# Three PSUM banks for one layer's scores, and the causal zeroing cut into halves

## The chip, the cores and the metric

The kernel is one program on one core of a Trainium2 chip. The metric is the device time of one execution in microseconds (us).

## The reference

The input x is 8 batches of 512 rows by 128 columns. Two layers follow each other, each with a layer normalisation ahead of it and x added behind it. Cut to what matters:

```
# layer A (16 heads, head size 8, values of 32)
Q = heads(x); K = heads(x @ Wk + bk); V = heads(x @ Wv + bv)
attn = softmax(Q K^T + causal mask)
x + gelu(concat(attn @ V)) @ Wf + bf
# layer F (8 heads, size 64, 8 experts)
q = x @ w_q; k = x @ w_k; gates = sigmoid(x @ w_gate); sel = argmax(gates)
gm = onehot(sel) * gates
values = sum_e gm[e] * (x @ value_experts[e])
out = softmax(causal(q k^T / 8)) @ values
sum over heads and experts of gm[e] * (out @ output_experts[e])
```

## The kernel before

Five engines run written-out programs, ordered among themselves and held together by semaphores. The batches go one after the other: layer A's attention, its end (`turn`: gelu and projection back, L814), layer F's projections and expert values, layer F's attention. Work of neighbouring batches is woven in: during layer F's attention the first maximum units of the next batch's layer A run, and during layer A's attention the expert products (L698) of the layer F before.

Layer A's 16 heads make four groups of four. Softmax takes two passes. In the first a *maximum unit* is a score block (queries in the partitions) in one of the two banks ps_max0, ps_max1; VectorE takes maxima (L1310), ScalarE the sums of exponentials (L919). VectorE makes from both, for each query, minus maximum minus logarithm of the sum (L1315 on), TensorE transposes it (`maxima_transposed`, L626), ScalarE copies it to mt_a (`maxima`), and three DMAs on the SP queue carry it into rows of the stacked queries (L395). In the second pass a *score unit* (`score_unit`, L587) computes scores with the keys in the partitions; the rows just made are part of that matmul. ScalarE's exponential (`weights`, L970) brings it into pt, already normalised. Each group has three stages of four units (512, 384 and 256 + 128 columns), so a batch has 48 units in layer A. When all four heads of a stage are there, GpSimd zeroes what lies above the diagonal (L1177), and TensorE weighs the values with it (`weigh`, L678), one stage behind the scores.

Units 0 to 23 of layer A alternate between ps_exp0 and ps_exp1, so unit u waits for the exponential of unit u-2. From unit 24 (WIDE) on the maximum units are done and the two ps_max banks are scores' banks too. The bank ps_m0 is used for transposes and for one value tile. Maximum units of the last group are spread over score units 2 to 22 (LATE). Lists give the places of the products by score unit: STEPS_AT holds the steps at which VectorE makes a product's operand and TensorE does the product before it, PRODUCTS_AT further ones of TensorE, LAST_AT of VectorE. VALUE_AT and SUMS_AT place the value tiles and the last sums of layer F among the maximum units ahead of the scores.

Of the kernel before, what the change touches and what calls it, by code (L numbers as in the profile page):

```python
# [24 lines left out]
P = 128  # L25
# [81 lines left out]

SCORES_AT = 10

# [4 lines left out]

VALUE_AT = {2: 0, 3: 1, 5: 2, 7: 3}

# [54 lines left out]
def build(nc, x, wk, bk, wv, bv, wf, bf, wq, wkf, wg, ve, oe, ident, consts, out):  # L171
    ctx = ExitStack()
    with ctx:
# [124 lines left out]
        mrow = {k: [sem(f"mrow{k}{n}", 2 * 16 * MROWS[k]) for n in range(2)] for k in "AF"}  # L298
        causal, pv_done = K2("causal", NST, NST), K2("pv_done", NST, NST)
        sums_out = K2("sums_out", GROUPS - 1, GROUPS)  # L300
# [189 lines left out]
        def _(pe):  # L490
# [131 lines left out]
            def maxima_transposed(k, b, g):  # L622
                dst = free(k, "T", g, (t_done[k], b, g + 1))
                pe.wait_ge(neg_ready[k].sem, neg_ready[k].count(b, g + 1))
                if k == "A":
                    nc.tensor.transpose(dst[:].bitcast(BF16)[0:48, 0:P], nm_a[:, g % 2, :], ident_b[:]  # L626
                                        ).then_inc(t_ready[k].sem, 1)
                else:
                    nc.tensor.transpose(dst[0:16, 0:P], nm_f[:, g % 2, :], ident_sb[:]).then_inc(t_ready[k].sem, 1)

            def score_unit(k, b, g, s, j):

                u, h = (g * STAGES + s) * HG[k] + j, g * HG[k] + j
                if k == "A" and u in (WIDE + 2, WIDE + 3):
                    pe.wait_ge(max_done["A"].sem, max_done["A"].count(b, UNITS["A"]))
                elif u >= 2:
                    pe.wait_ge(exp_done[k].sem, exp_done[k].count(b, u - 3 if k == "A" and u >= WIDE + 4 else u - 1))
                elif k == "A":
                    pe.wait_ge(va.sem, va.count(b, T))
                else:  # L640
                    pe.wait_ge(chosen.sem, chosen.count(b, choices(T * E - 1 + u)))
# [75 lines left out]
            def attention_a(a):  # L717
# [3 lines left out]
                for n, (g, m) in enumerate(pre_units(a)):  # L721
                    if a > 0 and n < 2:
                        continue
# [4 lines left out]
                    if g == 2 and m == SCORES_AT:  # L728
                        rows_arrived(a, 0)
                        score_unit("A", a, 0, 0, 0)  # L730
                        score_unit("A", a, 0, 0, 1)
                    max_unit("A", a, g, m)
# [6 lines left out]
                for g in range(GROUPS):  # L739
                    if g > 0:  # L740
                        rows_arrived(a, g)
                    for s in range(STAGES):
                        n = g * STAGES + s
                        for j in range(HG["A"]):
                            u = n * HG["A"] + j
                            if u >= 2:
                                score_unit("A", a, g, s, j)
# [6 lines left out]
                            elif u in PRODUCTS_AT:  # L754
                                product(a - 1, PRODUCTS_AT[u])
                            if s == 1 and j == 0 and g + 1 < GROUPS:
                                maxima_transposed("A", a, g + 1)
                        if n > 0:
# [4 lines left out]
            def attention_f(f):  # L763
# [30 lines left out]
                if f + 1 < B:  # L794
                    value_a(f + 1, 0)
                    for g, m in pre_units(f + 1)[:2]:
                        if m == 0:
# [60 lines left out]
        def _(act):  # L858
# [27 lines left out]
            def maxima(k, b, g):  # L886
                act.wait_ge(t_ready[k].sem, t_ready[k].count(b, g + 1))
                src = ps_m[BANK[(k, "T", g)]]
                if mrow[k][g % 2].count(b, 16 * MROWS[k] * (g // 2)):
                    act.wait_ge(mrow[k][g % 2].sem, mrow[k][g % 2].count(b, 16 * MROWS[k] * (g // 2)))  # L890
                if k == "A":
                    copy(mt_a[:, g % 2, :], src[:].bitcast(BF16)[0:48, 0:P]).then_inc(t_done[k].sem, 1)
                else:
                    copy(mt_f[:, g % 2, :], src[0:16, 0:P]).then_inc(t_done[k].sem, 1)

# [77 lines left out]
            def attention(k, b):  # L973
                n_units = STAGES * HG[k]
                for g, m in pre_units(b) if k == "A" else ():
                    if g == 2 and m == SCORES_AT:
                        weights(k, b, 0, 0)
                        weights(k, b, 0, 1)
                    denominators(k, b, g, m)
# [14 lines left out]
                for g in range(GROUPS):  # L994
                    for s in range(STAGES):
                        n = g * STAGES + s
                        for j in range(HG[k]):
                            u, m = n * HG[k] + j, s * HG[k] + j
                            if k == "F" or u >= 2:
                                weights(k, b, n, j)  # L1000
# [12 lines left out]
                            if k == "F" and b + 1 < B:  # L1013
                                firsts(b + 1, u - 1)
                            if k == "A" and s == 1 and j == 0 and g + 1 < GROUPS:
                                maxima(k, b, g + 1)
                            if k == "F":
# [129 lines left out]
        def _(pool):  # L1147
# [23 lines left out]
            def attention(k, b):  # L1171
                for n in range(NST):
                    pool.wait_ge(exp_done[k].sem, exp_done[k].count(b, (n + 1) * HG[k]))
                    s0, m = (n % 2) * 4, 2 if n % STAGES == 2 else 1
                    v = pt[:, s0:s0 + HG[k], 0:m * P].rearrange("p h (m c) -> p h m c", c=P)

                    nc.gpsimd.affine_select(out=v, in_=v, compare_op=ALU.is_ge, fill=0.0, base=0,  # L1177
                                            pattern=[[0, HG[k]], [0, m], [1, P]], channel_multiplier=-1
                                            ).then_inc(causal[k].sem, 1)

# [405 lines left out]
```

## Time and profile before

| | |
|---|---|
| median of 3 runs | 1226.84 us (1225.18 to 1228.56) |
| profiled execution, its own time | 1228.14 us |
| its span | 1226.4 us |
| granted TensorE clock, mean | 0.996 |
| busy share TensorE, ScalarE, VectorE, GpSimd | 92%, 77%, 70%, 30% |
| one batch (533.4 to 678.1 of the span) | 144.7 us |
| selects of GpSimd (L1177) | 192 |

The page's busy shares are means over the span; a window or a list of waits shows one stretch. In a timeline row the bracket at the end is the idle time of the engine before it and what ended it. Batches are equal to within some tenths of a microsecond, so one stands for all.

### The profile page before, as it was taken

The page shows a single profiled execution, that of the slowest core. Times are in us where ns is not written, and L with a number is a line of the kernel's source. Part 1 is how long each engine was busy: PE and PEld are TensorE (multiplying, and loading weights), DVE is VectorE, ACT ScalarE, POOL GpSimd, SP SyncE. Part 2 cuts the span into 40 slices and gives each one's busy share as a digit, 9 for nine tenths or more (in the row PEclk, how much of TensorE's full clock was granted, in tenths as well). Part 3 has the DMA queues.
Part 4 walks back from the last instruction along what each step waited for, and adds up shares of the span by engine and source line. Part 5 has one row for each costly group of instructions (what it writes and reads, how often), then busy time and mean ns, then how long its engine had stood idle before and what let it go on. Part 6 is the DMA issues. An engine that isn't in the chain of part 4 may idle for free.

```text
span 1226.4 us, 20153 instructions
## 1 busy us (share of the span) xinstructions
PE 1130.3 (92%) x5846; PEld 644.6 (53%) x5846; DVE 862.7 (70%) x2715; ACT 941.2 (77%) x2639; POOL 364.0 (30%) x460
## 2 busy tenths in 40 slices
PE   5989998999989999899989999899998999989998
PEld 3536753376434764357543675347643575435743
DVE  5735867678765878569676687767876597856844
ACT  3985898858986789867997589876898578986751
POOL 1024314432234223252233421442232432323310
PEclk9999999999999999999999999999999999999999
DMA  5311232022210233003320123202231033300220
GB/s 192 72 69 48 50 108 64 5 61 69 83 53 4 71 87 98 11 3 79 106 71 11 47 51 106 64 5 62 78 88 38 4 79 89 87 3 26 56 71 9
DMA packets 43647, 72.75 MB, mean 59 GB/s; under 512 B 9664, under 2 KB 25408, under 8 KB 43216
## 3 DMA queue, kind: packets, MB, share of 16 engines
q1 hardware_dynamic: 42142, 66.95, 20.3%
q10 hardware_dynamic: 1394, 4.50, 1.4%
q8 instruction: 47, 0.77, 0.3%
q14 instruction: 64, 0.52, 0.1%
HBM read 45.34 MB, written 8.80 MB: 44 GB/s over the span
## 4 chain that ended last, share of the span: by engine, by line
PE 64%; ACT 15%; DVE 12%; issue 5%; DMA 2%; POOL 1%; SPq 1%; ACTq 0%; DVEq 0%; POOLq 0%
PE ps_m L698 15%; PE ps_o L678 10%; ACT masked L919 7%; ACT pt L970 6%; PE ps_max L587 5%; PE ps_exp L587 4%; DVE masked L1310 4%; PE ps_m L496 3%; PE ps_exp L589 3%; PE ps_exp L496 3%; PE ps_m L498 3%; PE ps_m L497 3%; PE ps_exp L498 2%; PE ps_max L814 2%; PE ps_exp L497 2%
## 5 line engine op out<-in xcount | busy, mean ns | idle before, releaser
L1310 DVE CUSTOM_DVE_ANT_0 masked<-ps_max,mask 128x512 f32<-128x512 f32 (+3 forms) x768 | 350.1, 487 | 169.5 <-PE ps_max L587 101.2
L919 ACT ACTIVATE masked<-masked,low 128x512 f32<-128x512 f32 (+3 forms) x768 | 423.1, 554 | 52.4 <-DVE low L1310 50.8
L1177 POOL TENSOR_SCALAR_AFFINE_SELECT pt<-pt 128x512 f32<-128x512 f32 (+2 forms) x192 | 143.6, 748 | 556.1 <-ACT pt L970 556.1
L970 ACT ACTIVATE pt<-ps_exp 128x384 f32<-128x384 f32 (+1 forms) x480 | 237.4, 517 | 75.7 <-PE ps_exp L587 48.3
L678 PE MATMUL ps_o<-pt,val 128*32 128x128 f32 (+6 forms) x1536 | 178.7, 445 | 6.8 <-POOL pt L1177 6.8
L698 PE MATMUL ps_m<-at,oe_sb 128*128 128x512 f32 x300 | 154.3, 601 | 1.9 <-DVE at L1361 1.8
L919 ACT ACTIVATION_READ_ACCUMULATOR masked<-masked,low 128x1 f32 x768 | 147.2, 192 | 0.0
L587 PE MATMUL ps_max<-s2k,s1q 72*128 72x512 bf16 (+3 forms) x512 | 121.7, 304 | 21.3 <-DVE low L1310 14.0
L1361 DVE TENSOR_TENSOR at<-osb,hots 128x512 f32<-128x512 f32 x150 | 103.2, 689 | 29.8 <-PE ps_m L698 29.8
L587 PE MATMUL ps_exp<-s1q,s2k 75*128 75x384 bf16 (+3 forms) x384 | 90.7, 304 | 30.8 <-ACT pt L970 30.5
L678 PEld LDWEIGHTS ps_o<-pt,val 128*32 128x32 f32 (+1 forms) x1536 | 51.7, 117 | 106.8 <-issue 75.2
L589 PE MATMUL ps_exp<-s1q,s1k 128*128 128x256 f32 (+2 forms) x256 | 97.1, 390 | 11.0 <-DVE val L1501 9.4
L587 PEld LDWEIGHTS ps_max<-s2k,s1q 72*128 72x128 bf16 x512 | 45.9, 98 | 109.0 <-DVE low L1310 56.5
L698 PE MATMUL ps_m<-kept,oe_sb 128*128 128x512 f32 x212 | 101.1, 596 | 0.0
L1191 POOL CAST s1q<-pt 64x512 fp32r<-64x512 f32 x64 | 41.9, 655 | 166.4 <-ACT pt L1059 163.6
L1501 DVE COPY_PREDICATED val<-osb,ps_m 128x512 f32<-128x512 uint32 x112 | 80.6, 738 | 8.2 <-ACT val L859 8.2
L587 PEld LDWEIGHTS ps_exp<-s1q,s2k 75*128 75x128 bf16 x384 | 28.1, 97 | 108.0 <-ACT pt L970 80.1
L589 PE MATMUL ps_max<-s1k,s1q 128*128 128x256 f32 (+2 forms) x256 | 82.1, 332 | 1.3 <-DVE low L1310 1.3
L589 PEld LDWEIGHTS ps_exp<-s1q,s1k 128*128 128x128 f32 x256 | 48.1, 188 | 65.1 <-issue 39.0
L590 PE MATMUL ps_exp<-s2q,s2k 66*128 66x256 f32 (+5 forms) x256 | 80.4, 325 | 0.0
L590 PE MATMUL ps_max<-s2k,s2q 128*128 128x256 f32 (+5 forms) x256 | 80.1, 324 | 0.0
L1501 DVE COPY_PREDICATED val<-osb,ps_exp 128x512 f32<-128x512 uint32 x112 | 78.3, 736 | 0.3 <-PE ps_exp L498 0.2
(188 smaller groups left out, 2019.4 us busy)
## 6 DMA issues: line engine op xcount, KB each, us to landing
hots<-hot_d SPq DMA_DIRECT2D x48, 256.0 KB, 4.8
s1q<-parts_q SPq DMA_DIRECT2D x96, 96.0 KB
s2k<-parts_k SPq DMA_DIRECT2D x93, 96.0 KB
s1q<-pt SPq DMA_DIRECT2D x64, 128.0 KB, 2.3
s1k<-pt SPq DMA_DIRECT2D x64, 128.0 KB, 2.3
hots<-hot_d ACTq DMA_DIRECT2D x16, 256.0 KB, 4.8
parts_q<-pt SPq DMA_DIRECT2D x24, 128.0 KB, 2.3
parts_k<-pt SPq DMA_DIRECT2D x24, 128.0 KB, 3.9
```

Source lines behind the costliest of these rows:

```text
L496: mm(dst, lh, rh, start=True, stop=False)
L587: return mm(dst, l1[0:n, h, l2], r1[0:n, h, r2], start=True, stop=True)
L589: mm(dst, l1[0][:, h, l2], r1[0][:, h, r2], start=True, stop=False)
L590: return mm(dst, l1[1][n, h, l2], r1[1][n, h, r2], start=False, stop=True)
L678: last = mm(ps_o[g % 2][j * w:j * w + w, qt * P:S], val[:, kt, h * w:h * w + w], pt[:, (n % 2) * 4 + j, c0:c1], start=kt == 0, stop=kt == 3)
L698: mm(ps_m[1][:], oe_sb[:, u], chosen_o(f, u), start=u == 0, stop=u == T * E - 1).then_inc(at_used.sem, 1)
L919: last = nc.scalar.activation(e, e, ACT.Exp, bias=low[:, g % 2, c:c + 1], scale=-1.0, accum_out=den[:, g % 2, c:c + 1])
L970: nc.scalar.activation(pt[:, (n % 2) * 4 + j, 0:c1 - c0], score_bank(k, u)[:, c0:c1], ACT.Exp).then_inc(exp_done[k].sem, 1)
L1177: nc.gpsimd.affine_select(out=v, in_=v, compare_op=ALU.is_ge, fill=0.0, base=0, pattern=[[0, HG[k]], [0, m], [1, P]], channel_multiplier=- ...
L1310: last = v.tensor_tensor_reduce(out=masked[:, u % JUNK, c0:c0 + w], in0=src[:, c0:c0 + w], in1=mask[:, S - w:S], scale=-1.0, scalar=POS, o ...
L1361: v.tensor_tensor(chosen_o(f, u), osb[:, u // E], hots[:, u // E, u % E].bitcast(F8), ALU.mult).then_inc(at_done.sem, 1)
L1501: v.copy_predicated(val[:, t].rearrange("p (h k) -> p h k", k=64), pick, ps_m[BANK[("F", "moe1", n)]][:].rearrange("p (h k) -> p h k", k=6 ...
```

## The change

Layer A's scores of units 0 to 23 go around three banks (ps_exp0, ps_exp1, ps_m0), those from unit 24 on around five. Three scores instead of two are computed ahead, three maximum units instead of two stand ahead of layer F's last weighing. The transposed maxima of groups 1 to 3 no longer have a bank of their own: they are written at column 384 of the bank of a score unit that has 384 columns, two units later than before, and ScalarE copies them once that score is written. Those of group 0 go to ps_exp0. The lists of products, value tiles and last sums are changed. GpSimd's select is cut in two for both layers: each half covers half of a stage's heads and waits only for their exponentials; a weighing waits for both.

```diff
+SCORE_BANKS = {"A": 3, "F": 2}
+BANK["A", "T", 0] = 2
-SCORES_AT = 10
+SCORES_AT, SCORES_FIRST = 10, 3
+BESIDE = ('A',)
+ROWS_WITH = {"A": 2, "F": 0}
-VALUE_AT = {2: 0, 3: 1, 5: 2, 7: 3}
+AHEAD = 3
+VALUE_AT = {3: 0, 4: 1, 6: 2, 8: 3}
-STEPS_AT += [("A", u) for u in (1, 2, 4, 7, 11, 15, 19, 23, 27, 31)]
+STEPS_AT += [("A", u) for u in (1, 3, 5, 7, 10, 13, 16, 19, 23, 27)]
-PRODUCTS_AT = {35: T * E - TURN - 1, 39: T * E - TURN}
-LAST_AT = {(36 + n if n else 33): T * E - TURN + n for n in range(TURN)}
+PRODUCTS_AT = {31: T * E - TURN - 1, 39: T * E - TURN}
+LAST_AT = {(35 + n if n else 31): T * E - TURN + n for n in range(TURN)}
-SUMS_AT = 8
+SUMS_AT = 10
...
-            return (ps_exp + ps_max)[u % 4] if k == "A" and u >= WIDE else ps_exp[u % 2]
+            if k == "A":
+                return (ps_exp + ps_max + ps_m[0:1])[(u - WIDE) % 5] if u >= WIDE else (ps_exp + ps_m[0:1])[u % 3]
+            return ps_exp[u % 2]
+        def rows_unit(k, g):
+            return ((g - 1) * STAGES + 1) * HG[k] + ROWS_WITH[k]
+        def transposed_at(k, g):
+            if g == 0 or k not in BESIDE:
+                return ps_m[BANK[(k, "T", g)]], 0
+            return score_bank(k, rows_unit(k, g)), 384
...
+            def score_bank_free(k, b, u):
                 if k == "A" and u in (WIDE + 2, WIDE + 3):
                     pe.wait_ge(max_done["A"].sem, max_done["A"].count(b, UNITS["A"]))
-                elif u >= 2:
-                    pe.wait_ge(exp_done[k].sem, exp_done[k].count(b, u - 3 if k == "A" and u >= WIDE + 4 else u - 1))
+                elif k == "A" and u >= WIDE + 4:
+                    pe.wait_ge(exp_done[k].sem, exp_done[k].count(b, u - 4))
+                elif u >= SCORE_BANKS[k]:
+                    pe.wait_ge(exp_done[k].sem, exp_done[k].count(b, u + 1 - SCORE_BANKS[k]))
...
-                pe.wait_ge(causal[k].sem, causal[k].count(b, n + 1))
+                pe.wait_ge(causal[k].sem, causal[k].count(b, 2 * n + 2))
...
                         for j in range(HG["A"]):
                             u = n * HG["A"] + j
-                            if u >= 2:
+                            if s == 1 and j == ROWS_WITH["A"] and g + 1 < GROUPS:
+                                maxima_transposed("A", a, g + 1)
+                            if u >= SCORES_FIRST:
                                 score_unit("A", a, g, s, j)
...
             def maxima(k, b, g):
-                act.wait_ge(t_ready[k].sem, t_ready[k].count(b, g + 1))
-                src = ps_m[BANK[(k, "T", g)]]
+                if g == 0 or k not in BESIDE:
+                    act.wait_ge(t_ready[k].sem, t_ready[k].count(b, g + 1))
+                else:
+                    act.wait_ge(s_ready[k].sem, s_ready[k].count(b, rows_unit(k, g) + 1))
+                src, c = transposed_at(k, g)
...
                 for n in range(NST):
-                    pool.wait_ge(exp_done[k].sem, exp_done[k].count(b, (n + 1) * HG[k]))
+                    for half_ in range(2):
+                        w = HG[k] // 2
+                        pool.wait_ge(exp_done[k].sem, exp_done[k].count(b, n * HG[k] + (half_ + 1) * w))
+                        s0, m = (n % 2) * 4 + half_ * w, 2 if n % STAGES == 2 else 1
+                        v = pt[:, s0:s0 + w, 0:m * P].rearrange("p h (m c) -> p h m c", c=P)
+
+                        nc.gpsimd.affine_select(out=v, in_=v, compare_op=ALU.is_ge, fill=0.0, base=0,
+                                                pattern=[[0, w], [0, m], [1, P]], channel_multiplier=-1
+                                                ).then_inc(causal[k].sem, 1)
```

## Rows read from the trace of the kernel before

**Rows 1.** Busy time of each engine over the span, from the page.
```profile
PE 1130.3 (92%) x5846; PEld 644.6 (53%) x5846; DVE 862.7 (70%) x2715; ACT 941.2 (77%) x2639; POOL 364.0 (30%) x460
```

**Rows 2.** Stretches: us, busy PE, PEld, DVE, ACT, POOL, clock, DMA share, GB/s.
```profile
637.00:649.00 12.00, 9.48 (x49) 3.37 (x47) 6.03 (x22) 10.06 (x33) 2.50 (x3) 1.00 0.08 24
649.00:661.70 12.70, 11.51 (x73) 4.09 (x69) 7.60 (x29) 11.50 (x34) 3.31 (x4) 1.00 0.01 1
661.70:678.10 16.40, 15.51 (x123) 6.00 (x122) 11.78 (x25) 13.26 (x29) 7.56 (x8) 1.00 0.02 6
```

**Rows 3.** Waits between 637 and 678.1: who waited for whom, total, times, longest.
```profile
PEld ps_exp L587 <- ACT pt L970: 9.8, 17, 1.3
...
ACT pt L970 <- PE ps_exp L587: 6.0, 7, 1.5
...
PEld ps_o L678 <- POOL pt L1177: 2.3, 3, 1.0
...
PE ps_o L678 <- POOL pt L1177: 0.9, 2, 0.7
```

**Rows 4.** Timeline of TensorE: start, us, what, idle time before it.
```profile
641.28 0.33 PE L587 MATMUL ps_exp<-s1q,s2k 75*128 75x384 bf16 x1
642.61 0.34 PE L587 MATMUL ps_exp<-s1q,s2k 75*128 75x384 bf16 x1 [1.00 <-ACT pt L970]
...
643.00 1.02 PE L698 MATMUL ps_m<-at,oe_sb 128*128 128x512 f32 x2
643.96 1.06 PE L678 MATMUL ps_o<-pt,val 128*32 128x512 f32 x8
644.95 0.50 PE L587 MATMUL ps_exp<-s1q,s2k 75*128 75x256 bf16 x4
```

**Rows 5.** Timeline of ScalarE in the narrow part, exponentials that waited.
```profile
645.39 0.49 ACT L970 ACTIVATE pt<-ps_exp 128x384 f32<-128x384 f32 x1 [1.49 <-PE ps_exp L587]
...
649.58 0.60 ACT L970 ACTIVATE pt<-ps_exp 128x512 f32<-128x512 f32 x1 [0.99 <-PE ps_exp L587]
...
657.36 0.87 ACT L970 ACTIVATE pt<-ps_exp 128x384 f32<-128x384 f32 x2 [0.56 <-PE ps_exp L587]
```

**Rows 6.** Timeline of all engines at the phase's end.
```profile
673.78 0.88 ACT L970 ACTIVATE pt<-ps_max 128x384 f32<-128x384 f32 x2
...
674.12 0.85 PE L678 MATMUL ps_o<-pt,val 128*32 128x384 f32 x8 [0.69 <-POOL pt L1177]
...
674.74 1.44 POOL L1177 TENSOR_SCALAR_AFFINE_SELECT pt<-pt 128x1024 f32<-128x1024 f32 x1 [0.67 <-ACT pt L970]
...
675.98 1.48 ACT L1033 ACTIVATE osb<-osb 128x1536 f32<-128x1536 f32 x1
...
676.23 0.86 PE L678 MATMUL ps_o<-pt,val 128*32 128x256 f32 x16 [0.20 <-POOL pt L1177]
...
677.98 0.50 PE L814 MATMUL ps_max<-wf_sb,osb 128*128 128x128 f32 x3
```

**Rows 7.** Groups of selects by form: busy us, mean ns, idle before them.
```profile
L1177 POOL TENSOR_SCALAR_AFFINE_SELECT pt<-pt 128x512 f32<-128x512 f32 x96 | 77.8, 810 | 301.5 <-ACT pt L970 301.5
...
L1177 POOL TENSOR_SCALAR_AFFINE_SELECT pt<-pt 128x1024 f32<-128x1024 f32 x32 | 38.9, 1215 | 74.6 <-ACT pt L970 74.6
...
L1177 POOL TENSOR_SCALAR_AFFINE_SELECT pt<-pt 128x256 f32<-128x256 f32 x64 | 26.9, 421 | 180.0 <-ACT pt L970 180.0
```

**Rows 8.** The maxima tile: instructions, their ns, and the time to landing.
```profile
L395 SPq DMA_DIRECT2D s1q<-mt_a x96: 502/589/1415, 44.8 to 1099.6; - x96
...
DMA to landing us min/median/max: 1.6/1.7/6.1
```

**Rows 9.** Timeline around the last transposed maxima of layer A.
```profile
662.87 0.34 PE L587 MATMUL ps_exp<-s1q,s2k 75*128 75x384 bf16 x1
...
663.69 0.26 ACT L859 ACTIVATE mt_a<-ps_m 48x128 bf16<-48x128 bf16 x1
...
668.22 0.61 PE L587 MATMUL ps_exp<-s1q,s2k 75*128 75x512 bf16 x2
```

More of the change, by code:

```diff
@@ L640, in score_unit @@
                 else:
-                    pe.wait_ge(chosen.sem, chosen.count(b, choices(T * E - 1 + u)))
+                    pe.wait_ge(chosen.sem, chosen.count(b, choices(min(T * E - 1 + u, T * E))))
+            def score_unit(k, b, g, s, j):
+                u, h = (g * STAGES + s) * HG[k] + j, g * HG[k] + j
+                score_bank_free(k, b, u)
                 dst = score_bank(k, u)
@@ L721, in attention_a @@
                 for n, (g, m) in enumerate(pre_units(a)):
-                    if a > 0 and n < 2:
+                    if a > 0 and n < AHEAD:
                         continue
@@ L729, in attention_a @@
                         rows_arrived(a, 0)
-                        score_unit("A", a, 0, 0, 0)
-                        score_unit("A", a, 0, 0, 1)
+                        for j in range(SCORES_FIRST):
+                            score_unit("A", a, 0, 0, j)
                     max_unit("A", a, g, m)
@@ L755, in attention_a @@
                                 product(a - 1, PRODUCTS_AT[u])
-                            if s == 1 and j == 0 and g + 1 < GROUPS:
-                                maxima_transposed("A", a, g + 1)
                         if n > 0:
@@ L794, in attention_f @@
                 if f + 1 < B:
-                    value_a(f + 1, 0)
-                    for g, m in pre_units(f + 1)[:2]:
+                    for n, (g, m) in enumerate(pre_units(f + 1)[:AHEAD]):
+                        if n == 2:
+                            value_a(f + 1, 0)
                         if m == 0:
@@ L886, in maxima @@
             def maxima(k, b, g):
-                act.wait_ge(t_ready[k].sem, t_ready[k].count(b, g + 1))
-                src = ps_m[BANK[(k, "T", g)]]
+                if g == 0 or k not in BESIDE:
+                    act.wait_ge(t_ready[k].sem, t_ready[k].count(b, g + 1))
+                else:
+                    act.wait_ge(s_ready[k].sem, s_ready[k].count(b, rows_unit(k, g) + 1))
+                src, c = transposed_at(k, g)
                 if mrow[k][g % 2].count(b, 16 * MROWS[k] * (g // 2)):
@@ L891, in maxima @@
                 if k == "A":
-                    copy(mt_a[:, g % 2, :], src[:].bitcast(BF16)[0:48, 0:P]).then_inc(t_done[k].sem, 1)
+                    copy(mt_a[:, g % 2, :], src[:].bitcast(BF16)[0:48, 2 * c:2 * c + P]).then_inc(t_done[k].sem, 1)
                 else:
-                    copy(mt_f[:, g % 2, :], src[0:16, 0:P]).then_inc(t_done[k].sem, 1)
+                    copy(mt_f[:, g % 2, :], src[0:16, c:c + P]).then_inc(t_done[k].sem, 1)
             def repeat_hots(f, p):
@@ L976, in attention @@
                     if g == 2 and m == SCORES_AT:
-                        weights(k, b, 0, 0)
-                        weights(k, b, 0, 1)
+                        for j in range(SCORES_FIRST):
+                            weights(k, b, 0, j)
                     denominators(k, b, g, m)
@@ L998, in attention @@
                             u, m = n * HG[k] + j, s * HG[k] + j
-                            if k == "F" or u >= 2:
+                            if k == "A" and s == 1 and j == ROWS_WITH[k] and g + 1 < GROUPS:
+                                maxima(k, b, g + 1)
+                            if k == "F" or u >= SCORES_FIRST:
                                 weights(k, b, n, j)
@@ L1014, in attention @@
                                 firsts(b + 1, u - 1)
-                            if k == "A" and s == 1 and j == 0 and g + 1 < GROUPS:
-                                maxima(k, b, g + 1)
                             if k == "F":
@@ L1172, in attention @@
                 for n in range(NST):
-                    pool.wait_ge(exp_done[k].sem, exp_done[k].count(b, (n + 1) * HG[k]))
[L1174 to L1179, printed above, removed]
+                    for half_ in range(2):
[6 more added lines that the diff above has]
+                                                ).then_inc(causal[k].sem, 1)
             def copy_rows(f, p):
```

14 lines of the change are left out of this document (8 added, 6 removed).

## The prediction

> **What bounds the kernel now.** I read the page's line of busy times first [rows 1]: TensorE has work in it for 92% of the span, ScalarE for 77%, VectorE for 70% and GpSimd for 30%. An average of that kind does not say which engine a stage waits for, so I cut one of the eight batches into stretches [rows 2]. The change lives in layer A's score phase, in which every score matmul (L587) writes a PSUM bank, ScalarE takes the exponential out of it (L970), GpSimd zeroes what lies above the diagonal (L1177), and TensorE weighs the values with it (L678). In the batch shown this phase runs from 637.0 to 678.1. In its narrow part (units 2 to 23, with two banks for the scores) ScalarE is busy 10.06 of 12.0 us and then 11.50 of 12.7 us, TensorE 9.48 and 11.51 [rows 2]. Neither is full; they take turns. The waits of the phase say why [rows 3]: TensorE's weight loads for scores stood 9.8 us waiting for exponentials to free a bank, and ScalarE's exponentials stood 6.0 us, in seven waits, for scores to arrive. Two engines that wait for each other are short of buffers between them.
>
> How such a wait arises is in the timeline of TensorE [rows 4]. Unit 6's score starts at 641.28. Unit 7's starts only at 642.61, because with two banks it needs the exponential of unit 5. Behind unit 7 in TensorE's order stand a product (643.00) and the weighing of the stage before (643.96), so unit 8's score comes at 644.95. ScalarE runs dry meanwhile and idles 1.49 us before unit 8's exponential at 645.39 [rows 5]. The same happens before units 12 (0.99 us) and 20 (0.56 us) [rows 5]: 3.04 us of the 6.0. The other four waits, 3.0 us together, lie in the wide part (units 24 to 47, already with four banks). There TensorE waits for no exponential; it is full with scores, products and weighings, and its own work sets the pace.
>
> The phase's end is a chain [rows 6]: last exponentials 673.78 to 674.66, the zeroing of four heads at once 674.74 to 676.18, the last weighing at 676.23, then the back projection (L814) at 677.98. Beside it ScalarE, behind its last exponential, loads a table and applies the first gelu from 675.98 to 677.46, which L814 also needs. What follows L814 is paced by TensorE, so a shift of that start moves the batch.
>
> **The change part by part.** *Third bank, narrow part.* Unit u's score now waits for the exponential of u-3. Unit 7 then needs unit 4's exponential, which unit 6 needed before; it can follow right behind unit 6 and its maximum unit, about 641.45 instead of 642.61. The product, weighing and unit 8 follow 1.16 us earlier, and of the 1.49 us idle 0.33 is left before anything else has moved. The 0.99 and 0.56 have the same form and are smaller than one ScalarE unit of work (ScalarE's 21.6 us of narrow work over 22 units make about 1.0 us each), so one bank more covers them. The gain is bounded by 0 below (TensorE merely queues) and 3.04 above (ScalarE never idle). Is TensorE fast enough for the upper end? It has 24.7 us in the narrow part [rows 2] and of these ScalarE's bound is 21.6 (10.06 + 11.50). TensorE's busy sum is 20.99, in which the ends of pipelined matmuls are counted too, and it gets one more product. So both are nearly balanced and some turn-taking stays. I take 2.5 of the 3.04.
>
> *Products moved.* Ten steps at u = 1, 2, 4, 7, 11, 15, 19, 23, 27, 31 become 1, 3, 5, 7, 10, 13, 16, 19, 23, 27, and the extra products at 35 and 39 become 31 and 39. Counted by parts: the wide part had products at 27, 31, 35, 39 and now has them at 27, 31, 39, and the narrow part has one more. A product occupies TensorE from 643.00 until the weighing starts at 643.96, less the gap before it: 0.86 us. In the wide part that is off the pacing engine, in the narrow part it lies in TensorE's former waits. Between 0 and 0.86; I take 0.8. The fifth bank of the wide part removes a wait that isn't there: nothing.
>
> *Zeroing in halves.* Twelve selects of a layer become 24. The forms give the prices [rows 7]: 4x128 columns take 810 ns in the mean, 2x128 take 421, 4x256 take 1215. The first half starts two exponentials earlier, so only the second lies behind the last exponential: 421 instead of 810 ns, and 810 instead of 1215 where the form is wide. GpSimd's total rises by (2 x 421 - 810) = 0.03 to (2 x 810 - 1215) = 0.41 us a stage; for layer F's forms no row shows one head of 128 columns, its price lies between 0 and 421. GpSimd is busy 30%, and its selects waited for exponentials, so the additional time is covered by its idle time. Only five weighings of the phase waited for GpSimd, 3.2 us of queue time and idle [rows 3], most of it at the end: 0.69 us before 674.12 and 0.20 before 676.23 [rows 6]. The last select took 1.44; with a half of 0.81 the last weighing comes 0.63 us earlier and L814 could start at 677.35, but the gelu ends at 677.46. So the tail gains at most about 0.5; I take 0.45, at the least 0.
>
> [...]
>
> *Maxima through a score bank.* The transposed maxima of groups 1 to 3 (L626) are written beside the score of unit j = 2 of the second stage, two units later than now, and ScalarE copies them out only when that score is written. Then three DMAs carry them to the rows that the next group's first score needs. In the wide part this is tight: unit 28's score at 662.87, the copy at 663.69, unit 36's score at 668.22 [rows 9]. The copy moves behind one more exponential, 0.4 us or a little more. Three issues of 0.59 us each put the last 1.2 us behind the first, and 1.7 us later it has landed [rows 8]: 663.69 + 0.5 + 0.27 + 1.2 + 1.7 = 667.4. The need moves to 668.22 - 0.86 = 667.4. I expect 0 to 0.3 us of a new wait in this group and take 0.1; In groups 1 and 2 the need (unit 12, unit 24) comes at the earliest when four more units have passed ScalarE, 3.9 us behind the copy's start, and the rows take 0.27 + 1.2 + 1.7 = 3.2: enough.
>
> [...]
>
> *The rest.* The third maximum unit ahead of the last weighing of layer F, the value tiles one unit later, the sums of layer F two units later and the first three scores at once keep their amount of work. They move between 622 and 637, where VectorE's maxima and ScalarE's sums set the pace and not TensorE. Nothing, at worst 0.3 us a batch either way. The cap in layer F's wait names the same count.
>
> **The sum.** 2.5 + 0.8 + 0.45 - 0.1 = 3.65 us, and a little for units 24 on, which may start up to one ScalarE unit sooner since unit 24 needs unit 21's exponential instead of unit 22's: 3.8 us a batch. Batch 0 has the same phase. 8 x 3.8 = 30 us. The profiled execution took 1228.14 us (span 1226.4), so it becomes 1198; against the median of the three runs, 1226.84, it is 1196.5.
>
> **The rivals.** *Half the gain.* TensorE and ScalarE stay coupled elsewhere: the late maximum units need VectorE and a junk slot, and rows arrive late. Then the narrow part gives 1.3, the move 0.5, the tail 0.2, less 0.1: 1.9 us, 1212. For it speaks that both engines have nearly the same load; against it, that every wait I removed names the bank.
> *No change.* TensorE is at 92% and what it waited for was hidden. Then 1227. Against it speak ScalarE's 6.0 us of idle time at the very waits in question.
> *Slower: rows late.* One maxima landing took 6.1 us instead of 1.7 [rows 8]. If landings behind the later copy took that long, group 3's first score would wait 4.4 us, those of groups 1 and 2 4.4 - 0.7 = 3.7 each: 11.8 - 3.8 = 8.0 us slower a batch, 1290. It decides from a landing of about 3.4 us on, where the three waits together reach 3.8. Against it: DMA is nearly idle in these stretches (share 0.01 to 0.08 [rows 2]).
> *More than forecast.* All upper ends together: 3.04 + 0.86 + 0.5 + 0.4 = 4.8, 1188; and beyond that only if the front part gains too.
>
> **How the numbers follow.** Forecast (1188 to 1204) 0.55, half the gain (1204 to 1219) 0.25, beyond 1188 0.05, no change within 0.3% 0.07, slower 0.08. A measurement of this kernel tells some 0.3% from no change. Faster is then 0.85. The range reaches from 1187 to 1218 and leaves out a little under 2 in 10.
>
> **What would show it.** In the changed profile: waits of ScalarE's exponentials for scores in the phase down from 6.0 to about 2 us, and those of score weight loads for exponentials from 9.8 to under 5; ScalarE's busy share in the narrow part above 93% (87% now); 384 selects, of 421 and about 810 ns in layer A; L814 paced by the gelu; a batch about 3.8 us shorter. A wait of a score on the maxima's DMA of more than 0.5 us, or VectorE in the place of the bank as the releaser of scores, would prove me wrong.

## The result

The changed kernel takes 1187.37 us, median of 4 runs (1187.03 to 1188.24), against 1226.47 for the kernel before beside it. The ratio is 0.9675, with a 95% interval from 0.9663 to 0.9686, so it is faster by 39 us (39.1 by the medians, 39.9 by the ratio). The forecast was 30 us, 1196.5; the result lies at the lower edge of the range, 1187 (0.9675 of the 1226.84 that the forecast started from is 1187.0). Direction and place were right and the size was not: 39.1 / 8 = 4.9 us a batch where 3.8 were expected. The page's busy line after, beside [rows 1]:

```profile
PE 1120.6 (94%) x5846; PEld 649.6 (55%) x5846; DVE 863.0 (73%) x2715; ACT 938.4 (79%) x2639; POOL 399.6 (34%) x652
```

The work is the same but for GpSimd, whose selects became 384 and cost 35.6 us more. The time came out of idle stretches. To see which, I cut one batch of each kernel (the fifth) at five starts on TensorE: the last score matmul of layer F, the first score of layer A, the first score of unit 24, the last score of layer A, and the projection back (L814 before, L848 after). The stretches between them are called front, narrow, wide and tail below. The stretches view of the kernel before, then of the kernel after, columns as in [rows 2]:

```profile
621.43:634.38 12.95, 11.38 (x53) 5.23 (x52) 11.37 (x44) 11.73 (x42) 9.51 (x9) 1.00 0.50 127
634.38:660.26 25.88, 21.87 (x121) 7.86 (x119) 15.39 (x59) 22.78 (x72) 4.91 (x6) 1.00 0.05 13
660.26:673.21 12.95, 12.95 (x101) 5.20 (x97) 8.62 (x16) 9.81 (x25) 4.73 (x6) 1.00 0.01 3
673.21:677.98 4.77, 3.88 (x32) 1.36 (x30) 3.83 (x13) 4.74 (x9) 3.67 (x3) 1.00 0.05 14
```

```profile
601.26:613.74 12.48, 10.96 (x53) 5.33 (x52) 11.43 (x45) 11.76 (x44) 9.30 (x9) 1.00 0.58 131
613.74:635.99 22.25, 21.75 (x123) 8.60 (x121) 16.89 (x59) 22.05 (x70) 5.30 (x11) 1.00 0.06 15
635.99:648.02 12.03, 12.03 (x98) 4.82 (x95) 7.77 (x16) 10.12 (x26) 6.16 (x11) 1.00 0.02 3
648.02:652.76 4.74, 3.88 (x33) 1.35 (x29) 3.67 (x12) 4.71 (x9) 3.38 (x4) 1.00 0.04 14
```

The batch gained 0.47 in the front, 3.63 in the narrow part, 0.92 in the wide part and 0.03 in the tail: 5.05 us. In batches 3 and 7 (counted from 0) the wide part gives 0.4 to 0.5 less, as shown below. Layer F's projections and attention moved by 0.1 us at most (48.4 and 39.8 us before, 48.4 and 39.7 to 39.8 after).

Read the narrow rows. ScalarE is busy 22.05 of 22.25 us, 99%, and was busy 22.78 of 25.88, 88%. TensorE's 21.75 of 22.25 hardly leave room either; which of the two sets the pace is told by e3_old_products below. In the wide rows TensorE fills both stretches, and its stretch is shorter because one product is gone. The waits of the narrow stretch after:

```profile
DVE masked L1349 <- PE ps_max L608: 4.6, 6, 1.2
PEld ps_m L608 <- ACT pt L1007: 2.4, 5, 0.8
PEld ps_exp L608 <- ACT pt L1007: 1.6, 4, 0.6
PEld ps_o L711 <- POOL pt L1216: 1.5, 2, 0.8
...
PEld ps_exp L653 <- ACT pt L1007: 1.3, 2, 0.8
...
PE ps_exp L608 <- ACT pt L1007: 0.4, 2, 0.2
```

No line of the whole list, from which these are taken, has ScalarE waiting for a score; before, the same stretch had three such waits with 3.0 us [rows 5]. What is left waits the other way: TensorE is ahead, and its loads wait for the exponential that frees a bank. That is the picture of a stretch that ScalarE paces.

### The profile page after: what moved, and what is told of

It reads as the page before. It is cut to its first block, busy times and chain, and to the rows that moved or that the text cites. A ratio compares the mean times of both kernels' runs of the same rounds, so it can differ in the third digit from the quotient of the medians.

```text
span 1185.9 us, 20345 instructions
## 1 busy us (share of the span) xinstructions
PE 1120.6 (94%) x5846; PEld 649.6 (55%) x5846; DVE 863.0 (73%) x2715; ACT 938.4 (79%) x2639; POOL 399.6 (34%) x652
## 4 chain that ended last, share of the span: by engine, by line
PE 65%; ACT 15%; DVE 9%; issue 5%; DMA 2%; POOL 1%; SPq 1%; ACTq 0%; DVEq 0%; POOLq 0%
PE ps_m L731 14%; PE ps_o L711 10%; ACT masked L956 7%; ACT pt L1007 6%; PE ps_max L608 5%; PE ps_exp L610 3%; PE ps_exp L517 3%; PE ps_m L517 3%; PE ps_exp L519 3%; PE ps_exp L518 3%; PE ps_m L519 3%; PE ps_m L518 3%; PE ps_max L610 3%; PE ps_max L611 3%; PE ps_max L848 2%
## 5 line engine op out<-in xcount | busy, mean ns | idle before, releaser
L1216 POOL TENSOR_SCALAR_AFFINE_SELECT pt<-pt 128x256 f32<-128x256 f32 (+2 forms) x384 | 181.7, 475 | 477.5 <-ACT pt L1007 477.1
L1007 ACT ACTIVATE pt<-ps_exp 128x384 f32<-128x384 f32 (+1 forms) x400 | 202.1, 518 | 31.0 <-PE ps_exp L611 25.1
L731 PE MATMUL ps_m<-at,oe_sb 128*128 128x512 f32 x300 | 154.3, 601 | 1.8 <-DVE at L1400 1.8
L1400 DVE TENSOR_TENSOR at<-osb,hots 128x512 f32<-128x512 f32 x150 | 107.0, 714 | 15.9 <-PE ps_m L731 15.8
L731 PE MATMUL ps_m<-kept,oe_sb 128*128 128x512 f32 x212 | 101.5, 597 | 0.0
L610 PEld LDWEIGHTS ps_exp<-s1q,s1k 128*128 128x128 f32 x256 | 48.4, 189 | 64.5 <-issue 38.3
L608 PE MATMUL ps_exp<-s1q,s2k 75*128 75x512 bf16 (+3 forms) x272 | 64.8, 305 | 4.0 <-ACT pt L1007 4.0
L1349 DVE DVE_READ_ACCUMULATOR2_ANT low<- 128x1 f32 x768 | 65.0, 85 | 0.0
```

What stands on the lines that cost most here:

```text
L608: return mm(dst, l1[0:n, h, l2], r1[0:n, h, r2], start=True, stop=True)
L610: mm(dst, l1[0][:, h, l2], r1[0][:, h, r2], start=True, stop=False)
L731: mm(ps_m[1][:], oe_sb[:, u], chosen_o(f, u), start=u == 0, stop=u == T * E - 1).then_inc(at_used.sem, 1)
L1007: nc.scalar.activation(pt[:, (n % 2) * 4 + j, 0:c1 - c0], score_bank(k, u)[:, c0:c1], ACT.Exp).then_inc(exp_done[k].sem, 1)
L1349: last = v.tensor_tensor_reduce(out=masked[:, u % JUNK, c0:c0 + w], in0=src[:, c0:c0 + w], in1=mask[:, S - w:S], scale=-1.0, scalar=POS, o ...
L1400: v.tensor_tensor(chosen_o(f, u), osb[:, u // E], hots[:, u // E, u % E].bitcast(F8), ALU.mult).then_inc(at_done.sem, 1)
```

## The experiments

Each kernel is the changed one with one edit, unless another base is named. The ratio is to the kernel before, timed beside it; the stretches are means over batches 1 to 6 (the changed kernel: front 12.48, narrow 22.24, wide 12.12, tail 4.74; before: 12.96, 25.87, 12.95, 4.77).

**e1_two_banks: the third bank alone taken back.**

```
-SCORE_BANKS = {"A": 3, "F": 2}
+SCORE_BANKS = {"A": 2, "F": 2}
-... if u >= WIDE else (ps_exp + ps_m[0:1])[u % 3]
+... if u >= WIDE else ps_exp[u % 2]
```

> The changed kernel with its third bank taken back: units 0 to 23 again alternate between two banks, all else stays changed. Theory A (the bank carries the gain): the narrow part, which took 25.9 us before and 22.2 after, goes back to about 25.5, so 8 x 3.3 = 26 us are lost and the kernel takes 1213 us or so, with TensorE's score loads again waiting some 8 us a batch for exponentials. Theory B (the other edits, placed better, carry it together): less than 10 us are lost, 1190 to 1197.

Measured 1216.89 us, ratio 0.9916 [0.9899, 0.9933]. The bank is worth 0.0241 of 1226.7, 29.6 us: theory A, with some 4 us more than it said. Narrow 26.04 in the mean (27.4 in batch 3, 25.7 to 25.9 in the other five), everything else as in the changed kernel. In the stretches view the narrow part of the batch shown shows the idle time of ScalarE back, 2.92 us of 25.88:

```profile
630.50:656.38 25.88, 22.19 (x123) 8.46 (x121) 16.29 (x59) 22.96 (x71) 6.05 (x12) 1.00 0.05 13
```

**e6_bank_alone: the third bank without the other edits** (whole selects, the old places of the products and the old front, as in the three experiments that follow, together).

```
+ the edits of e2_whole_selects, e3_old_products and e4_old_front
```

> The banks alone: three banks for units 0 to 23, five from 24 on, the maxima beside a score; product lists, front and whole selects as in the kernel before. Taking the bank out of the changed kernel cost 29.5 us. Theory A (the parts add up): the bank alone brings as much, 1226.7 - 29.5 = 1197, give or take 2. Theory B (the bank needs the other edits, the moved product above all): 1202 or more.

Measured 1199.22, ratio 0.9774 [0.9760, 0.9788]: 27.7 us faster than before. Narrow 22.45, wide 12.95, front 12.95, tail 4.77. The bank alone thus gives 3.42 us a batch in the narrow part, and the fifth bank of the wide part gives nothing there, as forecast. ScalarE fills 99% of the narrow part in this kernel too:

```profile
619.49:641.94 22.45, 21.12 (x120) 8.07 (x119) 15.28 (x59) 22.26 (x71) 4.11 (x5) 1.00 0.05 14
```

**e3_old_products: products back at their old places.**

```
-STEPS_AT += [("A", u) for u in (1, 3, 5, 7, 10, 13, 16, 19, 23, 27)]
+STEPS_AT += [("A", u) for u in (1, 2, 4, 7, 11, 15, 19, 23, 27, 31)]
-PRODUCTS_AT = {31: T * E - TURN - 1, 39: T * E - TURN}
-LAST_AT = {(35 + n if n else 31): T * E - TURN + n for n in range(TURN)}
+PRODUCTS_AT = {35: T * E - TURN - 1, 39: T * E - TURN}
+LAST_AT = {(36 + n if n else 33): T * E - TURN + n for n in range(TURN)}
```

> The changed kernel with the product lists of before (steps, extra products, VectorE's last ones). Theory A (one product less in the wide part is worth its 0.86 us there, and the narrow part is set by ScalarE, so nothing comes back): 7 us lost, 1194. Theory B (the lists also decide how TensorE gets through the narrow part): over 10 us lost, 1198 or more. If the move is worth nothing: 1187.

Measured 1192.69, ratio 0.9719 [0.9701, 0.9738]: 0.0044, 5.4 us, lost. Wide is 12.95 again, and narrow stays at 22.25 with one product less in it. Its stretches view, narrow and wide part:

```profile
613.59:635.84 22.25, 21.11 (x120) 8.07 (x119) 16.53 (x58) 22.03 (x70) 6.08 (x11) 1.00 0.06 16
635.84:648.79 12.95, 12.95 (x100) 5.13 (x97) 8.16 (x16) 10.16 (x26) 6.15 (x11) 1.00 0.01 3
```

TensorE's busy time in the narrow part is 0.64 less and the stretch no shorter: there the product lies beside ScalarE's work, and in the wide part it costs its full length, 0.91 (12.95 against 12.04 in most batches).

**e4_old_front: the front as before.**

```
-SCORES_AT, SCORES_FIRST = 10, 3
+SCORES_AT, SCORES_FIRST = 10, 2
-AHEAD = 3
-VALUE_AT = {3: 0, 4: 1, 6: 2, 8: 3}
-SUMS_AT = 10
+AHEAD = 2
+VALUE_AT = {2: 0, 3: 1, 5: 2, 7: 3}
+SUMS_AT = 8
(and value_a(f + 1, 0) ahead of the loop over the next batch's maximum units)
```

> The changed kernel with the front of before: two scores and two maximum units ahead, value tiles and last sums at their old places. Between layer F's last score and layer A's first one the changed kernel gained 0.5 us a batch, which I had forecast as nothing. Theory A (that comes from these edits): 0.5 us a batch and perhaps the third early score, 4 to 6 us lost, 1191 to 1193. Theory B (it is only a shift between the landmarks, units 0 to 2 being closer together): 0 to 1 us lost, 1187 to 1188.

Measured 1191.0, ratio 0.9708 [0.9689, 0.9727]: 0.0033, 4.0 us, lost. Front 12.96, exactly the old value, and narrow 22.48, 0.24 longer (0.48 + 0.24 = 0.72 a batch, 5.8 us; the interval of the ratio holds it). Where the front's 0.48 comes from is in the timeline of all engines, first before, then after:

```profile
623.13 0.69 DVE L1310 CUSTOM_DVE_ANT_0 masked<-ps_max,mask 128x512 f32<-128x512 f32 x1
...
623.73 0.50 PE L496 MATMUL ps_o<-wv_h,xh 128*128 128x512 f32 x1
...
624.52 0.50 PE L587 MATMUL ps_max<-s2k,s1q 72*128 72x256 bf16 x3
...
625.01 0.43 DVE L1310 CUSTOM_DVE_ANT_0 masked<-ps_max,mask 128x256 f32<-128x256 f32 x1 [1.19 <-ACT masked L919]
```

```profile
602.96 0.69 DVE L1349 CUSTOM_DVE_ANT_0 masked<-ps_max,mask 128x512 f32<-128x512 f32 x1
...
603.56 0.50 PE L608 MATMUL ps_max<-s2k,s1q 72*128 72x256 bf16 x3
...
603.82 0.48 PE L517 MATMUL ps_o<-wv_h,xh 128*128 128x512 f32 x1
...
604.05 0.42 DVE L1349 CUSTOM_DVE_ANT_0 masked<-ps_max,mask 128x256 f32<-128x256 f32 x1 [0.39 <-PE ps_max L608]
```

VectorE takes the maxima nearly back to back in this part (busy 11.37 of 12.95 us before, 11.43 of 12.48 after), which fits the prediction's reading that it paces it. But before, it stood 1.19 us ahead of the operation at 625.01. The row names ScalarE as what ended that wait. The distance to TensorE says otherwise: the maximum scores start at 624.52 before and at 603.56 after, and VectorE's operation follows 0.49 us later in both. They were late because the first value tile (L496, 623.73) stood ahead of them in TensorE's order; after the change it stands behind them (L517, 603.82). The hole shrinks from 1.19 to 0.39 us. The experiment takes back four edits together, so that the time is shown to come from them, and that the value tile's place is the one that counts is read from the timelines alone.

**e2_whole_selects: one select a stage.**

```
-for half_ in range(2):
-    w = HG[k] // 2
+for half_ in range(1):
+    w = HG[k]
(causal counts NST again; TensorE waits for n + 1)
```

> The changed kernel with one select for each stage again, in both layers. Theory A (the halves hardly help: in the tail both halves of the last select run beside VectorE's operand products and take 1.1 us each, so the last half ends as late as the whole one did): 0 to 2 us lost, 1187 to 1190. Theory B (the halves free the weighings earlier as forecast, 0.45 us a batch and more inside the phase): 4 to 8 us lost, 1191 to 1196.

Measured 1188.45, ratio 0.9683 [0.9665, 0.9702]. The difference of 0.0008, 1.0 us, is inside the intervals. Narrow 22.37 (0.13 longer), tail 4.76.

**e7_halves_alone: the kernel before with the selects halved.**

```
-pool.wait_ge(exp_done[k].sem, exp_done[k].count(b, (n + 1) * HG[k]))
+for half_ in range(2):
+    w = HG[k] // 2
+    pool.wait_ge(exp_done[k].sem, exp_done[k].count(b, n * HG[k] + (half_ + 1) * w))
...
```

> The kernel before with only the selects cut into halves, in both layers. My forecast's term: 0.45 us a batch, 1223. Theory A (both halves of the last select run beside VectorE's operands with two inputs in SBUF and end as late as the whole did): within 1 us of the kernel before, 1225.5 to 1227. Theory B (more instructions on GpSimd slow VectorE's operands): above 1228.

Measured 1227.0, ratio 0.9999 [0.9988, 1.0010]; tail 4.74 against 4.77. Alone, the halves give nothing that can be measured.

**e8_kept_late: VectorE's last elementwise products of two SBUF tiles moved behind the last select.** The operands 28 to 31 (`kept<-osb,hots`) are made only after the select of the last half.

```
+KEPT_LATE = 28
-if a > 0 and u in LAST_AT:
+if a > 0 and u in LAST_AT and LAST_AT[u] < KEPT_LATE:
...
+dve.wait_ge(causal["A"].sem, causal["A"].count(a, 2 * NST))
+for u in range(KEPT_LATE, T * E):
+    choose(a - 1, u)
```

> The changed kernel in which VectorE makes the last four of the product operands (28 to 31) only when the last select of layer A is done, so that VectorE is idle beside it. Theory A (contention between GpSimd's selects and VectorE's two-input operands keeps the tail from getting shorter): the halves of the last select take about 0.65 us instead of 1.1, the last weighing starts up to 0.8 us earlier, and the back projection gains until the gelu holds it, 0.4 us a batch: 1184. Theory B (the selects are slow for another reason): they stay at 1.1 us and the time at 1187, or rises, since the last gelu waits for the operands.

Measured 1185.76 us, 5 runs from 1183.01 to 1186.34, ratio 0.9659 [0.9643, 0.9674]. It is the fastest of all kernels run, but its interval overlaps that of the changed kernel, so the times alone don't tell them apart. The stretch does: the tail is 4.45 against 4.74 in the mean (4.40 in all batches but one, which has 4.68). The timeline of the changed kernel's end:

```profile
648.60 0.88 ACT L1007 ACTIVATE pt<-ps_max 128x384 f32<-128x384 f32 x2
648.78 2.17 POOL L1216 TENSOR_SCALAR_AFFINE_SELECT pt<-pt 128x512 f32<-128x512 f32 x2 [0.51 <-ACT pt L1007]
...
650.79 1.48 ACT L1070 ACTIVATE osb<-osb 128x1536 f32<-128x1536 f32 x1
...
651.01 0.86 PE L711 MATMUL ps_o<-pt,val 128*32 128x256 f32 x16 [0.77 <-POOL pt L1216]
...
651.80 1.12 PE L731 MATMUL ps_m<-kept,oe_sb 128*128 128x512 f32 x2
```

And that of e8_kept_late:

```profile
648.46 0.88 ACT L1008 ACTIVATE pt<-ps_max 128x384 f32<-128x384 f32 x2
648.65 1.40 POOL L1217 TENSOR_SCALAR_AFFINE_SELECT pt<-pt 128x512 f32<-128x512 f32 x2 [0.57 <-ACT pt L1008]
...
650.08 2.50 DVE L1401 TENSOR_TENSOR kept<-osb,hots 128x512 f32<-128x512 f32 x4 [1.81 <-POOL pt L1217]
...
650.10 0.86 PE L712 MATMUL ps_o<-pt,val 128*32 128x256 f32 x16
650.66 1.48 ACT L1071 ACTIVATE osb<-osb 128x1536 f32<-128x1536 f32 x1
...
652.29 0.68 PE L849 MATMUL ps_max<-wf_sb,osb 128*128 128x128 f32 x4 [0.27 <-ACT osb L1071]
```

From the start of the last pair of exponentials to the last weighing it is 2.41 us in the changed kernel (648.60 to 651.01) and 1.64 in this one (648.46 to 650.10). The groups by form of the same moments (busy us, mean ns), after and then e8_kept_late, where the selects and the products come from two windows, one behind the other:

```profile
L1400 DVE TENSOR_TENSOR kept<-osb,hots 128x512 f32<-128x512 f32 x3 | 2.5, 899 | 0.0
L1216 POOL TENSOR_SCALAR_AFFINE_SELECT pt<-pt 128x512 f32<-128x512 f32 x2 | 2.2, 1108 | 0.5 <-ACT pt L1007 0.5
```

```profile
L1217 POOL TENSOR_SCALAR_AFFINE_SELECT pt<-pt 128x512 f32<-128x512 f32 x2 | 1.3, 637 | 0.7 <-ACT pt L1008 0.6
...
L1401 DVE TENSOR_TENSOR kept<-osb,hots 128x512 f32<-128x512 f32 x4 | 2.5, 687 | 1.8 <-POOL pt L1217 1.8
```

Side by side a half takes 1108 ns and a VectorE product 899; apart they take 637 and 687. The weighing then comes 0.77 us sooner, but the projection back only 0.29, because it now waits for the gelu, which in both kernels starts 2.77 us behind the start of layer A's last score.

**e11_whole_and_late: one select a stage, and the late operands of e8_kept_late.**

```
+ the edits of e2_whole_selects and e8_kept_late
```

> One select for each stage again, but with VectorE's last four operands behind the last select. It tells what halves are worth without the contention. Theory A (contention alone took the halves' gain): the last select takes 1.08 us instead of 1.44, the last weighing starts some 0.4 us later than with late operands and halves (0.64 each), and the gelu hides a part of it: 1187 to 1189 against 1185.8 with halves. Theory B (halves are worth nothing even alone): 1186.

Measured 1188.09, ratio 0.9668 [0.9647, 0.9690]; tail 4.48, against 4.45 with halves. Its timeline at the end:

```profile
648.17 1.10 POOL L1217 TENSOR_SCALAR_AFFINE_SELECT pt<-pt 128x1024 f32<-128x1024 f32 x1 [1.08 <-ACT pt L1008]
...
649.33 0.86 PE L712 MATMUL ps_o<-pt,val 128*32 128x256 f32 x16 [0.27 <-POOL pt L1217]
649.42 1.48 ACT L1071 ACTIVATE osb<-osb 128x1536 f32<-128x1536 f32 x1
```

Even with the products apart from them the halves are worth 0.03 us in the tail, and the ratios of the two kernels don't tell them apart: the whole select takes 1.10 us, and the gelu, which runs from 649.42 to 650.90 and is needed by the projection back at 651.08, ends the stretch with either.

**e5_rows_first: the maxima rows two units earlier.**

```
-ROWS_WITH = {"A": 2, "F": 0}
+ROWS_WITH = {"A": 0, "F": 0}
```

> The changed kernel with the transposed maxima beside the first unit of a group's second stage (j = 0) instead of the third: transpose, copy and the three DMAs come two units earlier. In the changed kernel's profile score loads waited for these DMAs 5.9 + 1.0 + 0.8 us in all, the term that I had put at 0.1 us a batch. Theory A (that wait sits on the pacing TensorE of the wide part): some 0.7 us a batch come back, 1181 to 1183. Theory B (the wait is hidden, or the earlier transpose holds TensorE up for its bank or for VectorE's maxima): 1187 or more.

Measured 1187.66, ratio 0.968 [0.9666, 0.9695], the same as the changed kernel: theory B. Narrow is 0.3 longer, with a wait of TensorE of 0.41 us for VectorE's nm_a, which the transpose now reaches too soon, and wide is 0.12 shorter.

**e9_one_product_more, e10_one_and_late, e12_two_and_late: one or two more products out of the wide part**, the latter two with the late operands.

```
e9, e10: -STEPS_AT ... (1, 3, 5, 7, 10, 13, 16, 19, 23, 27), PRODUCTS_AT 31, 39, LAST_AT from 31
         +STEPS_AT ... (1, 3, 5, 7, 9, 11, 14, 17, 20, 23),  PRODUCTS_AT 27, 39, LAST_AT from 27
e12:     +STEPS_AT ... (1, 3, 5, 7, 9, 11, 13, 15, 18, 21),  PRODUCTS_AT 23, 39, LAST_AT from 23
```

> The changed kernel with one more product moved out of the wide part: products at units 27 and 39 there instead of 27, 31 and 39, and the steps of the narrow part closer together. Theory A (TensorE sets the wide part and ScalarE the narrow one, and TensorE still has waits in the narrow part): 0.8 us a batch, 1181. Theory B (the narrow part is by now as full on TensorE as on ScalarE, so that the product only changes its place): 1186 to 1188.

> One more product moved and VectorE's last four operands behind the last select. If the two edits act on different engines and places, their gains add up: 1187.4 - 6.5 - 2 = 1179. If the moved product brings nothing: as the late operands alone, 1185.8.

> Two more products moved out of the wide part (only the one at 39 is left there) and late operands. Theory A (TensorE still has room in the narrow part): 1173. Theory B (the room is used up with the first one; ScalarE then waits for scores in the narrow part): no faster than one product more with late operands, or slower.

Measured 1196.84 (0.9744 [0.9724, 0.9765]), 1195.36 (0.9731 [0.9712, 0.9750]) and 1195.2 (0.9729 [0.9711, 0.9747]): all slower than the changed kernel, by 6.6 to 8.5 us if the ratios are compared. No theory of e9_one_product_more and no sum of e10_one_and_late had foreseen that: the worst of them was that the product brings nothing. The stretches view of e9_one_product_more, narrow and wide part:

```profile
617.18:640.70 23.52, 23.00 (x125) 8.87 (x123) 17.41 (x60) 22.18 (x71) 5.29 (x11) 1.00 0.05 14
...
640.70:652.71 12.01, 11.31 (x97) 4.47 (x93) 7.33 (x15) 9.98 (x25) 6.31 (x11) 1.00 0.01 3
```

TensorE's busy time in the narrow part rises by 1.25 and the stretch by 1.27: what was free for the product of e3_old_products is paid for with the next, and with more than the 0.91 that a product takes. ScalarE now stands 1.2 us waiting for scores, so TensorE's order paces the stretch; one of its products also waits 0.2 for its operand. And the wide part of this batch is no shorter (12.01 against 12.03), though TensorE has 0.72 us less in it; in the mean it is 0.1 longer (12.22). Its waits there say what took the place:

```profile
PEld ps_max L608 <- DMA s1q<-mt_a: 1.0, 1, 1.0
...
PE ps_o L711 <- POOL pt L1216: 0.4, 1, 0.4
...
PE ps_max L608 <- DMA s1q<-mt_a: 0.3, 1, 0.3
```

A weighing waits 0.4 for its select and group 3's first score 0.3 for its rows: 0.7, as much as TensorE has less to do. With two products moved (e12) the wide part falls to 11.57, and the narrow part rises to 24.19: 1.95 for the two, 0.97 for each.

## Why the prediction was right and where it was off

**The third bank: right place, too small.** This is the largest miss. The step that failed is "So both are nearly balanced and some turn-taking stays. I take 2.5 of the 3.04." Nothing of it stayed. ScalarE's timeline shows unit 0's and unit 24's exponentials, before and after:

```profile
636.33 1.05 ACT L970 ACTIVATE pt<-ps_exp 128x512 f32<-128x512 f32 x2
...
660.74 1.08 ACT L970 ACTIVATE pt<-ps_exp 128x512 f32<-128x512 f32 x2
```

```profile
615.51 1.06 ACT L1007 ACTIVATE pt<-ps_exp 128x512 f32<-128x512 f32 x2
...
636.86 1.07 ACT L1007 ACTIVATE pt<-ps_exp 128x512 f32<-128x512 f32 x2
```

From one to the other it is 24.41 us before and 21.35 after: 3.06 less, the whole of the three idle times 1.49, 0.99 and 0.56, that is, the upper bound. That TensorE has nearly as much work (21.75 us in 22.25) did not couple the two, because three banks let it run ahead of ScalarE. The bank alone, in e6_bank_alone, gave 3.42 a batch in the narrow part and 27.7 us in all; taken back, in e1_two_banks, it cost 29.6.

**Unit 24 a little sooner: right, and 0.39 to 0.57 instead of 0.15.** Measured on TensorE the narrow part shrank by 3.63, which is 0.57 more than on ScalarE. Unit 24's score starts 0.48 us ahead of its exponential before (660.26 to 660.74) and 0.87 after (635.99 to 636.86), 0.39 more lead, which the wide part inherits, since there TensorE sets the pace. The other 0.18 is at the start of the phase, where unit 0's score is 1.95 ahead of its exponential before and 1.77 after. I had bounded the term by ScalarE's idle time and forgot that the stretch handed over is TensorE's.

**The products: right.** Forecast 0.8 within 0 and 0.86. The wide part went from 12.95 to 12.12 in the mean, 0.83, with the loss by the rows in it; by itself the product is worth 0.91 (12.04 in the batches without that loss), a little over the bound. e3_old_products gives the same back; it was free in the narrow part, as argued. The runs e9 to e12 show what was not forecast: this was the last product that could be had so.

**The front: put at nothing, worth 0.48.** The failed step is "They move between 622 and 637, where VectorE's maxima and ScalarE's sums set the pace and not TensorE. Nothing". VectorE has work of the same length before and after (11.37 and 11.43 us), which fits that it sets the pace, but it had a hole of 1.19 us in its run, and the hole ended with a maximum unit that TensorE issued behind a value tile. The trace before has it; the prediction rests on no row of VectorE there. The term would have been bounded by 0 and 1.19. e4_old_front gives it back to the hundredth.

**The tail: 0.03 instead of 0.45.** Two things were wrong in it. The halves were priced at their form's mean (810 by [rows 7]), and in the changed kernel the form takes 772 in the mean, but the two that matter take 1108 beside VectorE's products (`kept<-osb,hots`). Two of these, one behind the other, end 1.47 us behind the last exponential (650.95 against 649.48), where the whole select ended 1.52 behind it [rows 6]. e8_kept_late, which takes the products away from them, shows what they add: 637 ns a half apart against 1108 together. Instruction by instruction, in the batch shown, a product starts at 648.74, the first half at 648.78 (1.13 us), the next product at 649.34 (1.12), the second half at 649.87 (1.08): each of the last three starts while the one before it runs and is lengthened by 0.43 to 0.50 against its length apart (0.64 and 0.69). Why the two hold each other up the runs don't show. In batch 5 ScalarE's last exponentials come 0.28 us later, and the weighing still starts 2.99 us behind the last score, as in batch 4: the product beside the last half sets that moment, and not the exponential. In batch 0, which has no products there, the halves take 0.64 in this kernel too. Secondly the weighing did not decide alone: with it 0.77 us sooner, the gelu lets the tail shrink by 0.29 and no more, and whole selects reach the same (e11_whole_and_late). So the halves gain in the tail only what the products beside them leave, and the gelu's floor would have taken most of it: with the products away the tail is 4.40 with halves and 4.43 without, so that 0.37 and 0.34 were the most to be had of the forecast 0.45. In the narrow part the halves gave 0.13. A reading was wrong too, without effect on the sum: the five waits for GpSimd [rows 3] belong to three weighings, since a weight load and its matmul stand in the list one beside the other.

**The maxima rows: right.** Forecast a loss of 0.1 within 0 and 0.3 a batch; measured nothing in six batches and 0.5 and 0.4 in two, 0.11 in the mean. In the list of waits over the whole trace after, the line for the rows is:

```profile
PEld ps_max L608 <- DMA s1q<-mt_a: 5.9, 8, 1.2
```

That looks like 0.7 a batch, but in most batches the load of 0.6 lies in the 0.8 us that TensorE takes from a weighing to the next score in any case (0.79 after, from 642.25 to 643.04; 0.78 before). Only in batches 3 and 7 does TensorE itself idle; the timeline of batch 3:

```profile
502.12 0.85 PE L711 MATMUL ps_o<-pt,val 128*32 128x384 f32 x8
503.44 0.60 PE L608 MATMUL ps_max<-s1q,s2k 75*128 75x512 bf16 x2 [0.46 <-DMA s1q<-mt_a]
```

What is special in these two batches is a DMA issue: the second of the three takes 1.10 and 0.99 us instead of 0.59, and the last row lands 7.5 and 7.4 us behind unit 24's score, where it is 7.0 otherwise. The kernel before has slow issues in the same batches (1.42 and 0.71) and does not feel them, since it needs the rows only at 8.0. The changed kernel needs them at 7.05, so that 0.07 us are left in a usual batch; it was as tight as forecast. Moving the copy 0.65 us ahead, in e5_rows_first, did not help: there an issue takes 1.55 in both batches, and they lose 0.4 again. Why an issue is slow there the runs don't show.

By the letter a sign against the forecast did appear, a score's wait on this DMA of more than 0.5 us (the line has 1.2 as its longest), but only 0.46 and 0.32 of TensorE's time stood still by it. The rival in which the rows come late and decide did not occur; that it was near is seen in e9_one_product_more, where the rows become one of two waits that end a shortened wide part.

**The sum.** Measured a batch: narrow 3.06 + 0.57, wide 0.83 with the rows in it, front 0.48, tail 0.03, together 4.97 from the means over batches 1 to 6. Eight of these less one front (the first batch has no layer F ahead of it) are 39.3 us; the medians gave 39.1. Forecast: 3.8. Of the 1.17 missed, 0.56 is the discount on the bank, 0.42 the two ends of the narrow part, 0.48 the front and 0.13 the products with the rows (0.83 for 0.8 - 0.1); the tail takes 0.42 back. The 0.13 are 0.11 more for the product by itself, while the rows cost what was forecast, and rounding. With 4.97 the batch lies above the 4.8 of the rival *More than forecast*, all upper ends together, which had a chance of 0.05 beyond 1188. It came out much as that rival says: the bank at its upper end, and the front gaining too. Of the signs that I had named, ScalarE's share (99%, above 93) and its waits for scores (1.6 us in the phase, about 2) came out; the waits of score loads for exponentials in the phase fell from 9.8 to 6.1 only (2.7 for ps_exp, 2.6 for ps_m, 0.8 for ps_max), where I had said under 5. They were no sign of loss: they are how a TensorE that is ahead looks. The selects are 384, but their forms take 471 and 772 in the mean, not 421 and 810, the smaller one with layer F's in it. And the projection back (L848, 652.76) is paced by the last product behind the late weighing (L731, from 651.80), not by the gelu, which ends at 652.27.

## What to carry to other kernels

When two engines take turns through too few buffers and neither is full, one buffer more can give the whole idle time of the busier one, as it did here (3.06 us a batch), with the other at 98% of the stretch afterwards; then add what the handing over to the next stretch gains, measured on the engine that paces that one. Look for holes in the run of the pacing engine before you put an edit at nothing: what ends the hole is what an edit may move. And once two engines are both nearly full, a piece of work moved there can cost its full length or more (1.27 us here for 0.91), and the stretch that it left may be held by the next wait.

## What the runs showed of the hardware that was not expected

At the end of a batch a GpSimd select of 128x512 f32 takes 637 ns by itself and 1108 beside VectorE's products `kept<-osb,hots`, and these go from 687 to 899 in the mean. In the kernel before this was already in the last select of the batch, 1.44 us (1.10 in batch 0, which has no products beside it, and in e11_whole_and_late). Spread over two instructions the last select was held up twice here, by 0.47 us each, where the whole one was held up by 0.34.
